# A graph network on one core: six beats of preparation a superblock, and early products in two halves

## What is computed

```
h = relu(layernorm(x))
deg = count of edges by destination (+1: a loop for each node)
conv(h, W, b) = segment_sum((h @ W)[src] * dinv[src] * dinv[dst], dst) + b
x = x + conv(relu(conv(relu(conv(h, W1, b1)), W2, b2)), W3, b3)
h = relu(layernorm(x))
red = segment_sum(h[src] + relvectors[edge_type], dst)
x = x + gru_cell(red, h)
```

## Time and profile before

| | |
|---|---|
| median of three runs | 904.02 us |
| profiled execution | 906.02 us |
| its span, first to last instruction | 902.1 us |
| mean granted TensorE clock | 0.988 of 2.4 GHz |
| TensorE busy | 862.2 us |
| VectorE busy | 451.5 us |
| ScalarE busy | 290.3 us |
| GpSimd busy | 82.0 us |

### The profile page before, as it was taken

How to read it: one execution, slowest core, us unless ns; L and a number is a source line. 1 busy time by engine, 2 the same in 40 slices (tenths; PEclk the granted TensorE clock), 3 DMA queues, 4 the chain that set the end, 5 groups by cost and what they waited for, 6 DMA issues and landing times.

```text
span 902.1 us, 14157 instructions
## 1 busy us (share of the span) xinstructions
PE 862.2 (96%) x4870; PEld 480.5 (53%) x4870; DVE 451.5 (50%) x1139; ACT 290.3 (32%) x609; POOL 82.0 (9%) x244
## 2 busy tenths in 40 slices
PE   2689999999999999999999999999999999999996
PEld 1348666666666454444455444445464555555554
DVE  6966899999996211221041433227162233333336
ACT  3365667667675100110020201222231112222122
POOL 0210300111000055540000000000000000000000
PEclk9989999999999999999999999999999999999999
DMA  6100000000001400000000101112310000000001
GB/s 197 31 2 1 3 17 22 17 16 23 16 23 50 137 3 3 3 2 1 1 0 30 47 23 41 38 39 70 123 33 20 12 24 24 24 24 24 24 26 42
DMA packets 36998, 28.34 MB, mean 31 GB/s; under 512 B 12869, under 2 KB 35553, under 8 KB 36924
## 3 DMA queue, kind: packets, MB, share of 16 engines
q1 hardware_dynamic: 36252, 26.97, 9.9%
q10 hardware_dynamic: 672, 0.41, 0.2%
HBM read 17.56 MB, written 9.81 MB: 30 GB/s over the span
## 4 chain that ended last, share of the span: by engine, by line
PE 92%; DVE 4%; ACT 1%; issue 1%; SPq 0%; DMA 0%; DVEq 0%
PE ps L1258 43%; PE ps L918 13%; PE ps L815 8%; PE ps L1269 5%; PE ps L640 5%; PE ps L643 5%; PE ps L1287 2%; PE ps L648 2%; PE ps L651 2%; PE ps L899 2%; PE ps L867 1%; DVE node_b L927 1%; PE ps L855 1%; PE ps L887 1%; PE ps L627 1%
## 5 line engine op out<-in xcount | busy, mean ns | idle before, releaser
L1258 PE MATMUL ps<-count,node_b 128*128 128x512 f16 (+3 forms) x1400 | 270.5, 351 | 0.4 <-DVE node_b L1419 0.3
L1258 PEld LDWEIGHTS ps<-count,node_b 128*128 128x128 f16 (+2 forms) x1400 | 121.5, 97 | 142.3 <-issue 7.6
L918 PE MATMUL ps<-node_a,count 128*128 128x512 f16 x525 | 180.4, 381 | 0.2 <-DVE node_a L1041 0.2
L815 PE MATMUL ps<-node_b 128*128 128x175 f16 x808 | 163.6, 257 | 12.0 <-issue 7.8
L927 DVE TENSOR_TENSOR node_b<-node_b 128x1024 f16<-128x1024 f16 (+2 forms) x253 | 157.4, 671 | 0.0
L1127 ACT ACTIVATE count<-ps 128x500 f32 x202 | 123.0, 609 | 72.9 <-PE ps L815 68.5
L1258 PE MATMUL ps<-count,node_a 128*128 128x512 f16 (+2 forms) x700 | 134.7, 352 | 0.0
L815 PEld LDWEIGHTS ps<-node_b 128*128 128x128 f16 x808 | 79.9, 100 | 41.1 <-issue 11.5
L1258 PEld LDWEIGHTS ps<-count,node_a 128*128 128x128 f16 (+1 forms) x700 | 60.0, 97 | 73.9 <-issue 7.1
L1349 DVE SCALAR_TENSOR_TENSOR work<-ps,dinv,params 128x256 f32<-128x256 f32 (+1 forms) x25 | 12.0, 481 | 124.3 <-PE ps L1269 124.3
L667 DVE TENSOR_TENSOR node_a<-ps,node_a 128x512 f32<-128x512 f32 (+1 forms) x25 | 17.2, 690 | 94.1 <-PE ps L643 94.1
(11 more groups left out here) (211 smaller groups left out, 805.3 us busy)
## 6 DMA issues: line engine op xcount, KB each, us to landing
node_a<-in_x SPq DMA_DIRECT2D x4, 768.0 KB, 8.4
table_scratch<-agg SPq DMA_DIRECT2D x21, 128.0 KB, 1.8
node_b<-table_scratch SPq DMA_DIRECT2D x3, 768.0 KB, 6.5
xt<-x_scratch SPq DMA_DIRECT2D x16, 128.0 KB, 2.2
out<-scaled SPq DMA_DIRECT2D x16, 128.0 KB, 1.7
xt<-in_x SPq DMA_DIRECT2D x12, 128.0 KB, 2.0
params<-in_x SPq DMA_DIRECT2D x12, 128.0 KB, 2.1
x_scratch<-xt SPq DMA_DIRECT2D x12, 128.0 KB, 1.7
```

Source lines behind the costliest of these rows:

```text
L815: return PE.matmul(window(s)[:, :, keys], low, key_hot[k][:, j, :, i].rearrange("p (t w) -> p t w", w=SPAN), start=(s == 0 and j == 0), st ...
L918: last = PE.matmul(out_slot(u)[0:m, :], count[:, t, u * P:u * P + m], node_a[:, t, :, :].rearrange("p a d -> p (a d)"), start=(t == 0), st ...
L1258: last = PE.matmul(ps[:, b, 0:cols], nodes[0:k, t, part, f * P:(f + 1) * P], count[0:k, t, c * CHUNK:c * CHUNK + cols], start=(n == 0 and ...
```

## The change

Six beats go to a superblock instead of four, and the beats of several steps are renumbered: counts 24 to 23, weighting 28 to 26, scales 33 to 32, weighing 40 to 36, factors 42 to 38, low parts 48 still (now twelve beats after weighing). The histogram becomes part of beat 30 of TensorE. Early products start at superblock 13. Rank, source and carry rows of the first pair are made before the verdict's cast and its key rows right behind it. The offset words are loaded in five parts, three of them at superblocks 2, 4 and 6 ahead of TensorE's wait for rows. VectorE clears the last tile, before the low part of tile 23. Each early product of 512 columns becomes two of 256, both parts added in the same 256 columns of PSUM, and VectorE reads one sum a tile.

```diff
-OFFSET_LOADS, LAST_WORDS_AT = (11, 18, 12), 4
+OFFSET_LOADS, WORDS_AT = (11, 8, 7, 7, 8), (2, 4, 6)
-BEATS = 4
+BEATS = 6
...
+        def rank_and_source_rows(m):
+            k, two = m % PAIRS_KEPT, slice(BATCH * m, BATCH * (m + 1))
+            one_hot(rel_rank_hot[BATCH * m // GROUP % 2][:, :, m % 2, :, :], rel_rank_k[:, :, two], 0, WINDOW).then_inc(*dve_seq.up())
+            one_hot(low_hot[k], low_k[:, :, two], 0, P).then_inc(*dve_seq.up())
+            if m % 2 == 0:
+                n = min(GROUP, NS - BATCH * m) // 2
+                one_hot(carry_hot[BATCH * m // GROUP % 2][:, 0:n, :, :],
+                        carry_k[:, BATCH * m:BATCH * m + 2 * n].rearrange("p (m i) -> p m i", i=2), 1, T).then_inc(*dve_seq.up())
+        def key_rows(m):
+            one_hot(key_hot[m % PAIRS_KEPT], key_k[:, :, BATCH * m:BATCH * (m + 1)], 0, T * SPAN).then_inc(hot_made, 1)
...
             DVE.tensor_reduce(verdict[:, :], rules, AX_X, ALU.add).then_inc(verdict_summed, 1)
+            DVE.wait_ge(keys_out, 5)
+            rank_and_source_rows(0)
             DVE.wait_ge(judged, 1)
             DVE.tensor_copy(verdict_i[:, :], ps[0:1, 5, 0:1]).then_inc(verdict_in, 1)
+            key_rows(0)
...
-        COUNTS_AT = 24
+        COUNTS_AT = 23
-        WEIGHT_AT = 28
-        SCALE_AT = 33
+        HIST_AT = 30
+        WEIGHT_AT = 26
+        SCALE_AT = 32
         DEGREE_AT = 36
-        WEIGH_AT = 40
-        FACTORS_AT = 42
+        WEIGH_AT = 36
+        FACTORS_AT = 38
-        LOW_PART_AT = WEIGH_AT + 8
+        LOW_PART_AT = WEIGH_AT + BATCH * BEATS
-        PRODUCTS_FROM = (WEIGH_AT + T) // BEATS + 2
+        PRODUCTS_FROM = max((WEIGH_AT + T) // BEATS + 2, SETTLE_FIRST + 2)
...
         def out_slot(u):
-            return ps[:, OUT_BANK + u % OUT_SLOTS, :]
+            return ps[:, OUT_BANK + u % OUT_SLOTS, 0:D]
...
+                if s in WORDS_AT:
+                    offset_words.extend(load_offsets(2 + WORDS_AT.index(s)))
                 PE.wait_ge(hot_made, s // BATCH + 1)
                 if s + 1 >= RING:
                     PE.wait_ge(win_written, s + 2 - RING)
-                if s == LAST_WORDS_AT:
-                    offset_words.extend(load_offsets(2))
...
-                if s == WEIGHT_AT // BEATS + 1:
-                    PE.wait_ge(hist_due, 2)
...
+            if beat == HIST_AT:
+                PE.wait_ge(hist_due, 2)
...
-            last = PE.matmul(out_slot(u)[0:m, :], count[:, t, u * P:u * P + m], node_a[:, t, :, :].rearrange("p a d -> p (a d)"),
-                             start=(t == 0), stop=(t == T - 1), skip_group_check=True)
+            for part in range(2):
+                last = PE.matmul(out_slot(u)[0:m, :], count[:, t, u * P:u * P + m], node_a[:, t, part, :],
+                                 start=(t == 0 and part == 0), stop=(t == T - 1 and part == 1), skip_group_check=True)
...
             t = beat - LOW_PART_AT
+            if t == T - 2:
+                DVE.wait_ge(x_weighted, T)
+                DVE.memset(node_a[:, T - 1, :, :], 0.0).then_inc(tail_cleared, 1)
...
-            DVE.scalar_tensor_tensor(out=scaled[k][0:m, :], in0=out_slot(u)[0:m, D:2 * D], scalar=newt[0:m, 1, u:u + 1], in1=xt[1][0:m, :],
-                                     op0=ALU.mult, op1=ALU.add).then_inc(*dve_seq.up())
-            DVE.wait_ge(*dve_seq.now)
-            DVE.scalar_tensor_tensor(out=work[k][0:m, :], in0=out_slot(u)[0:m, 0:D], scalar=newt[0:m, 1, u:u + 1], in1=scaled[k][0:m, :],
+            DVE.scalar_tensor_tensor(out=work[k][0:m, :], in0=out_slot(u)[0:m, :], scalar=newt[0:m, 1, u:u + 1], in1=xt[1][0:m, :],
                                      op0=ALU.mult, op1=ALU.add).then_inc(conv_read, 1)
...
-                if u == 0:
-                    POOL.wait_ge(x_weighted, T)
-                    POOL.memset(node_a[:, T - 1, :, :], 0.0).then_inc(tail_cleared, 1)
```

More of the change, by code:

```diff
@@ L737, in program, with rows_for, pair_of @@
         HIGH_AT = LOW_AT + 2 * Q
-        WEIGHT_AT = 28
-        SCALE_AT = 33
+        HIST_AT = 30
+        WEIGHT_AT = 26
+        SCALE_AT = 32
         DEGREE_AT = 36
-        WEIGH_AT = 40
-        FACTORS_AT = 42
+        WEIGH_AT = 36
+        FACTORS_AT = 38
         AHEAD_ACT = 2
-        LOW_PART_AT = WEIGH_AT + 8
+        LOW_PART_AT = WEIGH_AT + BATCH * BEATS
         OUT_AT, OUT_ACT_AT, OUT_LOW_AT = 5, 3, 12
-        assert HIGH_AT < WEIGHT_AT and WEIGHT_AT // BEATS * BEATS + BEATS <= DEGREE_AT - BEATS and TURN_AT + T <= WEIGH_AT
+        def rows_for(beat):
+            return (beat // BEATS + 1) // BATCH
+        def pair_of(beat):
+            return beat // (BATCH * BEATS)
+        assert HIGH_AT < WEIGHT_AT and TURN_AT + T <= WEIGH_AT and WINDOW <= COUNTS_AT < HIST_AT < WEIGH_AT
+        assert all(pair_of(own) >= rows_for(of_pe) for own, of_pe in ((COLUMNS_OUT_AT, COLUMNS_AT), (WEIGHT_AT, COUNTS_AT), (DEGREE_AT, HIST_AT)))
         assert SCALE_AT + SCALE_STEPS <= FACTORS_AT < BEATS * ASIDES // (WINDOW - 1)
-        PRODUCTS_FROM = (WEIGH_AT + T) // BEATS + 2
+        PRODUCTS_FROM = max((WEIGH_AT + T) // BEATS + 2, SETTLE_FIRST + 2)
         early_products = [(u, t) for u in range(EARLY) for t in range(T)]
@@ L833, in build_pe @@
                         beside_pe(w)
-                if s == WEIGHT_AT // BEATS + 1:
-                    PE.wait_ge(hist_due, 2)
-                    for w in range(WINDOW):
-                        for q in range(Q):
-                            part, pair = divmod(w, WINDOW // 2)
-                            last = PE.matmul(HIST, low_of[q][part][0:lanes(q), pair // 2, :, pair % 2],
-                                             high_of[0:lanes(q), (q * WINDOW + w) // 2, :, w % 2],
-                                             start=(w == 0 and q == 0), stop=(w == WINDOW - 1 and q == Q - 1), skip_group_check=True)
-                    last.then_inc(degrees_done, 1)
                 for u, t in due[len(between):]:
@@ L900, in beside_pe @@
                 last.then_inc(x_weighted, 1)
+            if beat == HIST_AT:
+                PE.wait_ge(hist_due, 2)
+                for w in range(WINDOW):
+                    for q in range(Q):
+                        part, pair = divmod(w, WINDOW // 2)
+                        last = PE.matmul(HIST, low_of[q][part][0:lanes(q), pair // 2, :, pair % 2],
+                                         high_of[0:lanes(q), (q * WINDOW + w) // 2, :, w % 2],
+                                         start=(w == 0 and q == 0), stop=(w == WINDOW - 1 and q == Q - 1), skip_group_check=True)
+                last.then_inc(degrees_done, 1)
             if beat == COLUMNS_AT:
@@ L948, in build_dve @@
                     DVE.wait_ge(win_done, s0 - BATCH * (PAIRS_KEPT - 1))
[L949 to L954 removed]
+                if m:
+                    rank_and_source_rows(m)
+                    key_rows(m)
                 if m == 0:
@@ L1286, in layers_pe @@
                 for t in range(T):
-                    last = PE.matmul(out_slot(u)[0:m, :], count[:, t, u * P:u * P + m], node_a[:, t, :, :].rearrange("p a d -> p (a d)"),
-                                     start=(t == 0), stop=(t == T - 1))
+                    for part in range(2):
+                        last = PE.matmul(out_slot(u)[0:m, :], count[:, t, u * P:u * P + m], node_a[:, t, part, :],
+                                         start=(t == 0 and part == 0), stop=(t == T - 1 and part == 1))
                 last.then_inc(conv_done, 1)
```

19 lines of the change are left out of this document (7 added, 12 removed).

## The result

| kernel | runs | median us | lowest to highest |
|---|---|---|---|
| before | 20 | 905.54 | 903.44 to 906.91 |
| after | 20 | 906.47 | 904.54 to 908.80 |

The ratio after to before is 1.0013, with a 95% interval of 1.0007 to 1.0019: 1.2 us slower, a small but measurable loss. The forecast was 0.7 us faster, counted from a median of 904.02 in three runs; from the 905.54 of the twenty its 903.3 would be 904.8. The profiled execution of the kernel after took 907.98 us (span 904.1, mean granted clock 0.987), 1.5 above its median, and that of before 0.5 above its own.

A forecast was written before the change was run, and what follows sets the result against it. TensorE was taken to pace the kernel, VectorE close behind. A gain of 3.8 us less 3.1 for halved products made 0.7 us less: median 903.3 us from 904.02, range 896 to 911.

The forecast's parts named there:

- Six beats: Preparation up to weighing: fewer pairs of rows between beats, counts read at 52 us instead of 56.6.
- the clock may again fall: After TensorE idles 1.5 to 2 us at superblocks 2 and 6: bounds 0 and 3 us, taken as 0.
- the halves: Two 256-column products for each of 625 products: 5 ns fixed cost a pair, 3.1 us slower.
- Level at superblock 2: Before superblock 2: TensorE ready at 32.2 us, level with VectorE's pair 1 rows at 32.0.
- the step gains: From the first product to the counts: 4.6 us gained, mainly by not fully repeating the 2.64 gap and slow clock.
- The reduction: GpSimd's reduction after centring: centring ends near 47.3 us, its preparation by 52.8 if it starts without the maxima.
- rival C: GpSimd's reduction: its 5.45 us begin only when the maxima are ready, chain 5 us later, 908.3 us; chance 0.06.
- The clearing: Last tile cleared on VectorE before superblock 12: TensorE idle 2.4 us where 1.3 before, costing about 1 us.
- Rival A: Every product from superblock 13: large fixed part of a 256-column product; 17.5 ns costs 10.9 us, 911.1; chance 0.12.
- The steady stretch: TensorE's 188 superblocks and 522 products after preparation: 192.8 us, ending at 285.0 against 288.8, 3.8 us gained.
- Rival B: GpSimd's diagonal addition for tile 1 comes late: TensorE idles 2.3 us, 905.6 us; chance 0.18.
- Rival E: Weighing waits for the counts as before, so six beats change nothing: 3.8 turns to 0, 907.1 us; chance 0.06.

The follow-up runs named there:

- filled: Kernel after, plus products of 256 columns that nothing reads in TensorE's idling before superblocks 2, 6 and 12: 903.76 us, ratio to before 0.9976.
- start_filled: start_alone plus products of 256 columns that nothing reads ahead of superblocks 6, 8 and 10: 901.39 us, ratio to before 0.9959.
- rows_ahead: Kernel after, but VectorE makes the rows of pair m + 1 ahead of the beats of pair m: 903.08 us, ratio to before 0.9971.
- all_filled: rows_ahead with clearing back on GpSimd, maxima at beat 36, factors at 42, and unread products at superblock 6: 900.50 us, ratio to before 0.9943.
- all_filled_whole: all_filled with whole products of 512 columns and two readings of a sum: 905.34 us, ratio to before 0.9998.
- whole_products: Kernel after with whole products of 512 columns again and two readings of a sum: 905.32 us, ratio to before 1.0000.
- halves_alone: Kernel before with only the products cut into halves of 256 columns and one reading a tile: 906.95 us, ratio to before 1.0014.
- before_filled: Kernel before plus products of 256 columns that nothing reads ahead of superblocks 4, 8 and 10: 903.00 us, ratio to before 0.9977.
- start_alone: Kernel before with only the first pair's early rows and the offset words loaded in five parts: 902.13 us, ratio to before 0.9959.

## Why the prediction was wrong

**The failed step** is in "Six beats": "After idling of 1.5 to 2 us at superblocks 2 and 6 the clock may again fall: bounds 0 and 3 us; I take 0 and keep 3 in the range." The clock fell, at three places and not two, and what the fillers gave back was 3.3 us: the term was put at 0 and is 3.3. With it the forecast of 0.7 us faster would be 2.6 slower; less the 1.5 us by which the halves were priced too high it is 1.1 slower, and 1.2 was measured. That these two corrections close the sum so well is partly luck, since each is known to about 1 us. The timeline of the prediction is that of the kernel filled:

| step | predicted | after | filled |
|---|---|---|---|
| first source product | 24.5 | 24.0 | 24.3 |
| superblock 3 | 39.6 | 41.9 | 39.5 |
| superblock 4, behind its words | 46.7 | 48.8 | 46.2 |
| counts read by VectorE | 52 | 53.4 | 51.4 |
| fourth tile of weighing | 66.5 | some 69.7 | 66.2 |
| weighing done | 87.7 | 91.0 | 87.8 |
| superblock 12 | 90.1 | 93.4 | 90.2 |
| products of the last tiles | 287.6 | 290.4 | 287.0 |
| median of the runs | 903.3 (904.8 from 905.54) | 906.47 | 903.76 |

(The fourth tile after: six tiles end at 65.08 + 7.20, the last three at 0.87 each.) The lag of the kernel after behind filled is 2.4 us at superblock 3 already, and 3.2 at superblock 12.

**Level at superblock 2.** "Ready at 32.2, level with VectorE" had TensorE too late. Its first six beats end at 29.2, 0.53 us each; the 0.70 a beat, from 2.79 for four in the earlier trace rows, was the pace of TensorE's first microseconds of work. In the kernel before eight such products took 2.79 us at 28.54 and 1.49 at 32.31, though the granted clock reads 1.00 for both; in the kernel after three of them begin from 26 to 27 us, four from 27 to 28 and seven from 28 to 29. TensorE, having started earlier, got through the slow part sooner. What makes it slow isn't shown. VectorE's rows came as predicted (31.9). So the idling was 2.7 us and not near zero, and the column sums, which VectorE waits for, stood right behind it.

**The base.** The chain of the kernel before held two slow stretches itself (0.66 from 40 to 50 in the earlier trace rows; weighing 5.42 us for four tiles in the earlier trace rows against 3.48). Of the "4.6 us" that "the step gains" by six beats, 2.0 us are the earlier start (24.5 for 26.52), and a part is the first slow stretch. Six beats by themselves lose 3.3 us, and the gain is the start's; that attribution was wrong, though the times of its steps agree with filled. The prediction also took 0.5% for what a measurement can tell; with 20 runs of each kernel it was 0.06%.

**The reduction.** What goes ahead of it doesn't wait for the maxima: it came 5.71 us after centring, at 56.25, only 1.4 us after the maxima were ready (54.8); in filled 6.05 us after centring. So rival C was void. The reduction was late, as centring ended at 50.5 and not 47.3. In filled it ended at 48.2, so most of this is VectorE's wait for the slow column sums: the clock again.

**The clearing.** Predicted 2.4 us of idling, measured 2.5; priced at 1 us against before, measured 1.4 plus or minus 1.2. The half clock behind it wasn't in the price. That the same edit measured 3.7 plus or minus 1.5 with four beats fits this, but idling and clock weren't separated there.

**The halves.** Priced 5 ns a pair from the 53-column row, measured 2.5, so 1.6 us where 3.1 were forecast. Rival A was void. The steady stretch was right: 192.8 us and 522 pairs at 2.5 ns make 194.1, and from superblock 14 (96.3) to 290.36 it is 194.1. Rival B didn't occur: the addition for tile 1 took 0.43 us. Rival E is half true: six beats bring nothing, but the start does.

## What to carry to other kernels

Price an idle stretch of TensorE with the half clock behind it, and look at what work stands there: three stretches of 2.5 to 3 us cost the kernel after 3.3 us in all, beyond the idling. Where idling can't be removed, products that nothing reads were cheap and made the times of two kernels steadier too; to a third, start_filled, they gave nothing that can be told. Rows made a pair ahead of the other work gave as much in rows_ahead, and more together with two late places put back. Take a bundle of edits apart before judging it: here one of four gained 3.7 us and the others gave it back; and an edit that loses alone (one reading for two halves) can be worth 5 us in another order of work (all_filled against all_filled_whole).

## What was not expected of the hardware

Idle stretches of TensorE of 2.70, 2.99 and 2.48 us in the kernel after were each followed by half clock for some 3 to 10 us; 1.3 us in the kernel before were not, nor 2.3 us in rows_ahead, ahead of its first early product. And the same pause can go either way. Here is TensorE at superblock 12 in the kernel after and in whole_products (start, us, what, idling before it):

```profile
93.42 0.83 PE L848 MATMUL ps<-node_b 128*128 128x175 f16 x3 [2.48 <-DVE node_b L269]
```

```profile
92.48 0.75 PE L848 MATMUL ps<-node_b 128*128 128x175 f16 x3 [2.48 <-DVE node_b L269]
```

The window of whole_products there:

```profile
92.00:96.00 4.00, 3.46 (x25) 2.06 (x26) 4.00 (x9) 1.38 (x3) 0.00 (x0) 1.00 0.02 3
```

The idling is equal; the granted clock of 92 to 96 us was 0.61 in the kernel after and 1.00 in whole_products. A single profile shows where a kernel can lose the clock, not how often it does. The Trainium skill, page "TensorE: Matmul & The Clock Gate", section "What's actually happening", says that the slow clock is the default and that activity releases it. The trace of the kernel after agrees so far as the clock was 0.50 from 59 to 60 us, where TensorE did nothing, and came back to 1.00 at 69 us, while it worked. Over executions of the kernel before the mean was 0.986 to 0.993, and this goes with most of its spread of 4 us.

GpSimd's addition of the diagonal of tile 1 took 6.79 us before and 0.43 after. The long one is no accident of one execution: it took 6.7 to 6.8 us in the traces of before, halves_alone, before_filled, start_alone and start_filled, which all have four beats and the clearing on GpSimd, and it began some 3 us after that clearing ended. In no other of the traces did an addition take over 3.6 us. Why it is long there is not shown.
